# Cross-attention of a two-layer decoder: each head scaled and added to x by one VectorE operation from PSUM, in place of scaled heads in SBUF and a tree of sums on GpSimd

## The chip, the cores and the metric

The kernel runs on one core of one Trainium2 chip. The metric is the device time of one execution in microseconds, lower is better. Before the change the median of three runs is 790.59 us (788.66 to 793.35).

## The reference, cut to what matters

The program is a decoder of two layers on x of 8 batch items x 128 tokens x 128 channels. Each layer has three sublayers, each added to x: a state-space mixer or self-attention, a cross-attention, and a mixture of experts. The change is in the cross-attention, which both layers have. For each item and each of the 16 heads it computes

```python
attn = jax.nn.softmax(scores, axis=-1)
out = jnp.einsum('bhqk,bhkd->bhqd', attn, v)
out = out.transpose(0, 2, 1, 3).reshape(B, NQ, INNER)
return out @ w_out + b_out
```

and the result is added to x. In layer 1 a second, small attention over 4 image tokens is added to `out` ahead of the output product.

## The kernel before, in words

Each sublayer is a block in which all engines start together and which ends when all are done. All data of x (`pg.x`, 8 items of 128x128) stays in SBUF; the next block, the feed-forward, begins with the statistics of all items of x on VectorE.

`cross_attention` folds the value and output weights of each head into one 128-wide matrix, so that a head's output is already 128 channels of x: `vo` holds, for an item, 16 heads x (128 channels and two columns of ones). The product of the unnormalised softmax weights `pt` with `vo[head]` gives in PSUM a head's 128 output channels and, in column 128, its sum of weights. What is left is to divide each head by its sum, add the 16 heads, the bias and x.

A loop over j (items 0 to 7) does item j's second half together with projections and scores of items j + 1, j + 2. The 16 heads are taken in six groups, of 3, 3, 2, 3, 3 and 2 heads (`groups`, `first`), that alternate between the two PSUM banks of `av`: groups 0 to 2, then the transposed scores and exponentials of the second half (`scores_t(j, 2)`), then groups 3 to 5. TensorE's `outputs(j, g)` waits until the group two before it, k - 2, has been read from its bank. All engines work in program order and meet by semaphores, of which the order is written out by hand in the functions of each engine.

VectorE's `normalise` (L1243 to L1258) takes a group's reciprocals (L1248), then multiplies the whole group into the tile `o` (L1254, `o_done`). Behind groups 0 to 2 stands the norm of item j + 3, behind groups 3 to 5 the statistics of item j + 4 and the row maxima of item j + 2 (L1212), which free the banks of the scores. GpSimd adds the 16 heads in a tree (L892 to L906: part, total, total, ...) and the result to x (L911). In layer 1 VectorE adds the image part to x from PSUM behind group 5 (L1257).

Of the kernel before, what the change touches and what calls it, by code (L numbers as in the profile page):

```python
# [10 lines left out]
ALU = mybir.AluOpType  # L11
# [3 lines left out]
P = 128  # L15
NB = 8
D = 128
# [788 lines left out]
def cross_attention(pg, layer):  # L806
# [5 lines left out]
    with ExitStack() as ctx:  # L812
        (split_ready, var_ready, rstd_ready, norm_order, xn_ready, proj_ready, proj_read, wvt_ready, wvt_copied, g_ready,
         g_high_done, g_low_done, c_high_done, c_low_done, ones_done, s_ready, s_read, nm_ready, st_ready, exp_done, av_ready,
         rinv_done, o_done, img_out_added, half_done, sum_order, x_done) = pg.sems(f"ca{layer}", (
            "split_ready var_ready rstd_ready norm_order xn_ready proj_ready proj_read wv_transposed wv_t_copied g_ready "
            "g_high g_low c_high c_low ones_done s_ready s_read max_ready st_ready exp_done av_ready "
            "rinv_done o_done image_added half_summed sum_order x_done"))
# [13 lines left out]
        rinv, o = some(2, "rinv", [P, NH]), some(2, "o", [P, NH, D])  # L832
        part, total = sb("part", [P, 4, D]), sb("total", [P, 4, D])
# [37 lines left out]
        def _(pool):  # L871
# [15 lines left out]
            for j in range(NB):  # L887
                if j + 3 < NB:
                    rstd(j + 3)
                oj = o[j % 2]  # L890
                pool.wait_ge(o_done, NG * j + 3)
                nc.gpsimd.tensor_tensor(part[:, :, :], oj[:, 0:4, :], oj[:, 4:8, :], ALU.add).then_inc(half_done, 1)  # L892
                pool.wait_ge(o_done, NG * j + NG)
                if j:
                    pool.wait_ge(x_done, j)
                s = 5 * j
                nc.gpsimd.tensor_tensor(total[:, :, :], oj[:, 8:12, :], oj[:, 12:16, :], ALU.add).then_inc(sum_order, 1)  # L897
                pool.wait_ge(half_done, j + 1)
                pool.wait_ge(sum_order, s + 1)
                nc.gpsimd.tensor_tensor(total[:, :, :], total[:, :, :], part[:, :, :], ALU.add).then_inc(sum_order, 1)  # L900
                pool.wait_ge(sum_order, s + 2)
                nc.gpsimd.tensor_tensor(total[:, 0:2, :], total[:, 0:2, :], total[:, 2:4, :], ALU.add).then_inc(sum_order, 1)
                pool.wait_ge(sum_order, s + 3)
                nc.gpsimd.tensor_tensor(total[:, 0, :], total[:, 0, :], total[:, 1, :], ALU.add).then_inc(sum_order, 1)
                pool.wait_ge(sum_order, s + 4)
                nc.gpsimd.tensor_tensor(total[:, 0, :], total[:, 0, :], w["bias"][:, :], ALU.add).then_inc(sum_order, 1)  # L906
                pool.wait_ge(sum_order, s + 5)
                pool.wait_ge(xn_ready, j + 1)
                if layer:
                    pool.wait_ge(img_out_added, j + 1)  # L910
                nc.gpsimd.tensor_tensor(pg.x[:, j, :], pg.x[:, j, :], total[:, 0, :], ALU.add).then_inc(x_done, 1)  # L911

        @block.tensor
        def _(pe):
# [91 lines left out]
            def outputs(j, g):  # L1006
                k = NG * j + g
                if k >= 2:
                    pe.wait_ge(o_done, k - 1)
# [180 lines left out]
        def _(dve):  # L1190
# [52 lines left out]
            def normalise(j, g):  # L1243
                dve.wait_ge(av_ready, NG * j + g + 1)
                slots = slice(groups[g][0], groups[g][-1] + 1)
                size = len(groups[g])
                src = av[g % 2][:, 0:size * (D + 2)].rearrange("p (h e) -> p h e", e=D + 2)
                V.reciprocal(rinv[j % 2][:, slots].unsqueeze(2), src[:, :, D:D + 1]).then_inc(rinv_done, 1)  # L1248
                dve.wait_ge(rinv_done, NG * j + g + 1)
                if g == 0 and j >= 2:  # L1250
                    dve.wait_ge(half_done, j - 1)
                if g == 2 and j >= 2:
                    dve.wait_ge(sum_order, 5 * (j - 2) + 1)
                V.tensor_tensor(o[j % 2][:, slots, :], src[:, :, 0:D], bc(rinv[j % 2][:, slots].unsqueeze(2), [P, size, D]),  # L1254
                                ALU.mult).then_inc(o_done, 1)
                if layer and g == NG - 1:
                    V.tensor_tensor(pg.x[:, j, :], av[g % 2][:, 2 * (D + 2):2 * (D + 2) + D], pg.x[:, j, :],  # L1257
                                    ALU.add).then_inc(img_out_added, 1)  # L1258
# [844 lines left out]
```

## Time and profile before

| | |
|---|---|
| median of three runs | 790.59 us (788.66 to 793.35) |
| the profiled execution, its own time | 789.37 us |
| its span, first to last instruction | 787.6 us |
| TensorE busy | 672.5 us (85%) |
| VectorE busy | 391.5 us (50%) |
| ScalarE busy | 289.6 us (37%) |
| GpSimd busy | 194.2 us (25%) |
| mean granted TensorE clock | 0.902 of full |

The busy shares are means over stages with different limits. The cross-attention of layer 0 lies from about 115 to 256 us of the span and that of layer 1 from about 480 to 625 us. What the change is worth is read there: from what TensorE waits for in an item, and from what works last at the end of the block. In the rows DVE is VectorE, PE TensorE's matmuls, PEld its weight loads, ACT ScalarE, POOL GpSimd; a start and a length are in us.

### The profile page before, as it was taken

The numbers are of one execution on the slowest core, as the hardware profiler recorded it, in microseconds if no ns is written. First come the engines' busy times: TensorE is split into PE (matmuls) and PEld (weight loads), VectorE is DVE, ScalarE is ACT, GpSimd is POOL, SyncE is SP. The second block draws the span as 40 slices with busy tenths as digits, with TensorE's granted clock in tenths as the row PEclk, the third lists the DMA queues.
The fourth block names the chain that finished last, engine by engine and source line by source line (L and its number), as shares of the span: only waits on it lengthen the run. The fifth ranks groups of instructions, "written<-read, shape, count | busy, mean of one in ns | idle before, by whom it ended". The sixth has DMA issues, their size and how long they took to land. (4 is left out here: it accounts for less than half of the span.)

```text
span 787.6 us, 13686 instructions
## 1 busy us (share of the span) xinstructions
PE 672.5 (85%) x5200; PEld 554.2 (70%) x5200; DVE 391.5 (50%) x1034; ACT 289.6 (37%) x561; POOL 194.2 (25%) x263
## 2 busy tenths in 40 slices
PE   4395978999995799997899977899998399999997
PEld 2263556888884678886666656788887279999886
DVE  2348754454553655553565524356555354443443
ACT  2443314545442333222444324444543153232331
POOL 8306341243445100002010001034433521111110
PEclk9755978999999699998899958799999879999999
DMA  7800000000000111000000000000000111111110
GB/s 191 198 1 0 0 0 2 1 2 1 2 1 1 41 41 31 30 20 1 2 2 1 2 1 1 1 2 2 2 1 2 44 38 41 40 40 40 43 38 27
DMA packets 23461, 18.33 MB, mean 23 GB/s; under 512 B 5576, under 2 KB 20208, under 8 KB 23408
## 3 DMA queue, kind: packets, MB, share of 16 engines
q1 hardware_dynamic: 23408, 17.60, 8.1%
q8 instruction: 36, 0.59, 0.3%
q14 instruction: 17, 0.14, 0.1%
HBM read 16.68 MB, written 0.52 MB: 22 GB/s over the span
## 5 line engine op out<-in xcount | busy, mean ns | idle before, releaser
L1969 ACT ACTIVATE sb_ff_s<-bank 128x512 f32<-128x512 f32 x96 | 57.4, 598 | 145.4 <-PE bank L1892 144.9
L2038 DVE TENSOR_TENSOR sb_ff_h<-sb_ff_s,bank 128x512 f32<-128x512 f32 x96 | 66.0, 688 | 72.4 <-ACT sb_ff_s L1969 71.1
L1902 PEld LDWEIGHTS bank<-sb_ff_down,sb_ff_h 128*128 128x128 f32 x768 | 88.2, 192 | 1.3
L1902 PE MATMUL bank<-sb_ff_down,sb_ff_h 128*128 128x128 f32 x768 | 88.3, 275 | 0.0
L1892 PE MATMUL bank<-sb_ff_xt_high,sb_ff_low 128*128 128x512 f32 x192 | 79.0, 411 | 1.3 <-DVE sb_ff_h L2038 1.3
L1015 PE MATMUL bank<-sb_ca_vo,sb_ca_pt 128*128 128x130 f32 (+1 forms) x512 | 70.8, 281 | 7.8 <-ACT sb_ca_pt L1133 4.3
L1892 PE MATMUL bank<-sb_ff_xt_low,sb_ff_high 128*128 128x512 f32 x192 | 76.4, 398 | 0.0
L1892 PE MATMUL bank<-sb_ff_xt_high,sb_ff_high 128*128 128x512 f32 x192 | 76.4, 398 | 0.0
L1015 PEld LDWEIGHTS bank<-sb_ca_vo,sb_ca_pt 128*128 128x128 f32 (+1 forms) x512 | 64.2, 190 | 14.4 <-DVE sb_ca_o L1254 7.0
L2031 DVE SCALAR_TENSOR_TENSOR sb_x<-bank,sb_ff_cw,sb_x 128x128 f32<-128x128 f32 x128 | 36.0, 344 | 47.9 <-PE bank L1902 47.9
L1133 ACT ACTIVATE sb_ca_pt<-bank 128x512 f32<-128x512 f32 (+1 forms) x64 | 36.0, 594 | 63.8 <-PE bank L1001 63.8
L1212 DVE TENSOR_REDUCE sb_ca_m<-bank 128x4 f32<-128x512 f32 (+1 forms) x64 | 40.6, 676 | 31.5 <-PE bank L979 31.5
L1117 ACT COPY sb_ca_vo<-bank 128x512 f32<-128x512 f32 (+1 forms) x64 | 37.6, 587 | 50.6 <-PE bank L948 49.0
L1248 DVE RECIPROCAL sb_ca_rinv<-bank 128x3 f32<-128x3 f32 (+1 forms) x96 | 16.7, 174 | 76.9 <-PE bank L1015 68.8
L1254 DVE TENSOR_TENSOR sb_ca_o<-bank,sb_ca_rinv 128x384 f32<-128x384 f32 (+1 forms) x96 | 49.2, 513 | 3.3
L1852 POOL TENSOR_TENSOR sb_ff_low<-sb_ff_gate_up,sb_ff_high 128x1024 fp32r<-128x1024 f32 x8 | 19.2, 2400 | 108.5 <-ACT sb_ff_high L1947 108.5
L1892 PEld LDWEIGHTS bank<-sb_ff_xt_high,sb_ff_low 128*128 128x128 f32 x192 | 37.1, 193 | 9.3 <-DVE sb_ff_h L2038 2.1
L1892 PEld LDWEIGHTS bank<-sb_ff_xt_high,sb_ff_high 128*128 128x128 f32 x192 | 36.8, 192 | 8.4
L1892 PEld LDWEIGHTS bank<-sb_ff_xt_low,sb_ff_high 128*128 128x128 f32 x192 | 37.1, 193 | 7.1
L897 POOL TENSOR_TENSOR sb_ca_total<-sb_ca_o 128x512 f32<-128x512 f32 x16 | 20.3, 1269 | 84.3 <-DVE sb_ca_o L1254 84.3
L936 PE MATMUL bank<-sb_ctx_t,sb_c_k 96*128 96x128 f32 x256 | 35.9, 299 | 5.5 <-PEq L117 3.2
L936 PEld LDWEIGHTS bank<-sb_ctx_t,sb_c_k 96*128 96x128 f32 x256 | 33.1, 209 | 7.0 <-issue 3.7
(339 smaller groups left out, 1231.2 us busy)
## 6 DMA issues: line engine op xcount, KB each, us to landing
sb_ff_w<-in_L_ffn_w_dram SPq DMA_DIRECT2D x8, 256.0 KB, 2.8
sb_ff_gate_up<-in_L_ffn_w_gate_dram SPq DMA_DIRECT2D x8, 256.0 KB, 2.7
sb_ff_gate_up<-in_L_ffn_w_up_dram SPq DMA_DIRECT2D x8, 256.0 KB, 3.0
sb_ff_down<-in_L_ffn_w_down_dram SPq DMA_DIRECT2D x8, 256.0 KB, 3.8
sb_ff_w<-in_L_ffn_w_dram SPq DMA_DIRECT2D x8, 128.0 KB, 2.7
sb_x<-in_x_dram SPq DMA_DIRECT2D x1, 512.0 KB, 5.0
sb_c_q<-in_L_xattn_w_q_dram SPq DMA_DIRECT2D x1, 512.0 KB, 4.7
sb_c_o<-in_L_xattn_w_out_dram SPq DMA_DIRECT2D x1, 512.0 KB, 7.9
```

The lines of the kernel that those rows point to most:

```text
L897: nc.gpsimd.tensor_tensor(total[:, :, :], oj[:, 8:12, :], oj[:, 12:16, :], ALU.add).then_inc(sum_order, 1)
L936: mm = nc.tensor.matmul(proj[h][:, t * P:(t + 1) * P], w["k"][:, (4 * h + t) * P:(4 * h + t + 1) * P], pg.ctx_t[:, n, :], start=True, stop ...
L1015: mm = nc.tensor.matmul(av[g % 2][:, i * (D + 2):(i + 1) * (D + 2)], pt[0:KS, c, r * P:(r + 1) * P], vo[j % 2][0:KS, head(c, r), :], start ...
L1117: nc.scalar.copy(vo[n % 2][0:KS, 4 * q:4 * q + 4, 0:D], proj[q % 2][0:KS, :].rearrange("p (h d) -> p h d", d=D)).then_inc(proj_read, 1)
L1133: nc.scalar.activation(pt[0:KS, c, :], score_t[c % 2][0:KS, :], ACT.Exp).then_inc(exp_done, 1)
L1212: V.tensor_reduce(m[n % 2][:, heads_of(c)], s[:, :, 0:KS], AX, ALU.max, negate=True).then_inc(s_read, 1)
L1254: V.tensor_tensor(o[j % 2][:, slots, :], src[:, :, 0:D], bc(rinv[j % 2][:, slots].unsqueeze(2), [P, size, D]), ALU.mult).then_inc(o_done, 1)
L1892: mm = nc.tensor.matmul(ps[k % BK][:, :], wp[p][:, g, t * P:(t + 1) * P], xs[xp][:, cols], start=(q == 0), stop=(q == 2))
L1902: mm = nc.tensor.matmul(y_ps[n][:, b * D:(b + 1) * D], h[n][:, t, b * P:(b + 1) * P], down[p][:, t, :], start=(t == 0), stop=(t == FT - 1))
L1969: nc.scalar.activation(s[k % BK][:, :], gate_ps[k % BK][:, :], ACT.Silu).then_inc(act_done, 1)
L2031: ins = V.scalar_tensor_tensor(pg.x[:, n * TB + b, :], y_ps[n][:, b * D:(b + 1) * D], cw[:, e, n * TB + b:n * TB + b + 1], pg.x[:, n * TB ...
L2038: V.tensor_tensor(h[k // FT][:, k % FT, :], s[k % BK][:, :], up_ps[k % BK][:, :], ALU.mult).then_inc(h_done, 1)
```

## The change

VectorE's `normalise` becomes `accumulate`: after a group's reciprocals it issues, for each head of the group, one operation that reads the head from PSUM, multiplies it with the head's reciprocal and adds it to x[j], in place. As each reads what the one before wrote, it waits on the semaphore `summed` of the one before. TensorE's `outputs` waits on `summed` up to the last head of group k - 2 (in place of `o_done`). GpSimd's tree goes; it adds the bias to x[j] as soon as the norm of item j has been read (`xn_ready`), and the first group of an item waits for this (`bias_added`). The tiles `o`, `part` and `total` go.

```diff
@@ -885,30 +884,11 @@
             rstd(2)
             pg.wait_loads(pool, f"cross{layer}")
             for j in range(NB):
+
+                pool.wait_ge(xn_ready, j + 1)
+                nc.gpsimd.tensor_tensor(pg.x[:, j, :], pg.x[:, j, :], w["bias"][:, :], ALU.add).then_inc(bias_added, 1)
                 if j + 3 < NB:
                     rstd(j + 3)
-                oj = o[j % 2]
-                pool.wait_ge(o_done, NG * j + 3)
-                nc.gpsimd.tensor_tensor(part[:, :, :], oj[:, 0:4, :], oj[:, 4:8, :], ALU.add).then_inc(half_done, 1)
-                pool.wait_ge(o_done, NG * j + NG)
-                if j:
-                    pool.wait_ge(x_done, j)
-                s = 5 * j
-                nc.gpsimd.tensor_tensor(total[:, :, :], oj[:, 8:12, :], oj[:, 12:16, :], ALU.add).then_inc(sum_order, 1)
-                pool.wait_ge(half_done, j + 1)
-                pool.wait_ge(sum_order, s + 1)
-                nc.gpsimd.tensor_tensor(total[:, :, :], total[:, :, :], part[:, :, :], ALU.add).then_inc(sum_order, 1)
-                pool.wait_ge(sum_order, s + 2)
-                nc.gpsimd.tensor_tensor(total[:, 0:2, :], total[:, 0:2, :], total[:, 2:4, :], ALU.add).then_inc(sum_order, 1)
-                pool.wait_ge(sum_order, s + 3)
-                nc.gpsimd.tensor_tensor(total[:, 0, :], total[:, 0, :], total[:, 1, :], ALU.add).then_inc(sum_order, 1)
-                pool.wait_ge(sum_order, s + 4)
-                nc.gpsimd.tensor_tensor(total[:, 0, :], total[:, 0, :], w["bias"][:, :], ALU.add).then_inc(sum_order, 1)
-                pool.wait_ge(sum_order, s + 5)
-                pool.wait_ge(xn_ready, j + 1)
-                if layer:
-                    pool.wait_ge(img_out_added, j + 1)
-                nc.gpsimd.tensor_tensor(pg.x[:, j, :], pg.x[:, j, :], total[:, 0, :], ALU.add).then_inc(x_done, 1)
 
         @block.tensor
         def _(pe):
@@ -1006,7 +986,7 @@
             def outputs(j, g):
                 k = NG * j + g
                 if k >= 2:
-                    pe.wait_ge(o_done, k - 1)
+                    pe.wait_ge(summed, NH * ((k - 2) // NG) + first[(k - 2) % NG + 1])
                 if layer and g == 1 and j:
                     pe.wait_ge(img_out_added, j)
                 pe.wait_ge(exp_done, NCH * j + groups[g][-1] // HPC + 1)
@@ -1240,20 +1220,22 @@
                 V.tensor_tensor(s2[n % 2][:, :, :], s2[n % 2][:, :, :], bc(sum2[n % 2][:, :].unsqueeze(2), [P, NH, IPA]),
                                 ALU.mult).then_inc(p2_ready, 1)
 
-            def normalise(j, g):
+            def accumulate(j, g):
+
                 dve.wait_ge(av_ready, NG * j + g + 1)
+                if g == 0:
+                    dve.wait_ge(bias_added, j + 1)
                 slots = slice(groups[g][0], groups[g][-1] + 1)
-                size = len(groups[g])
-                src = av[g % 2][:, 0:size * (D + 2)].rearrange("p (h e) -> p h e", e=D + 2)
+                src = av[g % 2][:, 0:len(groups[g]) * (D + 2)].rearrange("p (h e) -> p h e", e=D + 2)
                 V.reciprocal(rinv[j % 2][:, slots].unsqueeze(2), src[:, :, D:D + 1]).then_inc(rinv_done, 1)
                 dve.wait_ge(rinv_done, NG * j + g + 1)
-                if g == 0 and j >= 2:
-                    dve.wait_ge(half_done, j - 1)
-                if g == 2 and j >= 2:
-                    dve.wait_ge(sum_order, 5 * (j - 2) + 1)
-                V.tensor_tensor(o[j % 2][:, slots, :], src[:, :, 0:D], bc(rinv[j % 2][:, slots].unsqueeze(2), [P, size, D]),
-                                ALU.mult).then_inc(o_done, 1)
+                for i, s in enumerate(groups[g]):
+                    if s:
+                        dve.wait_ge(summed, NH * j + s)
+                    V.scalar_tensor_tensor(pg.x[:, j, :], src[:, i, 0:D], rinv[j % 2][:, s:s + 1], pg.x[:, j, :], ALU.mult,
+                                           ALU.add).then_inc(summed, 1)
                 if layer and g == NG - 1:
+                    dve.wait_ge(summed, NH * j + NH)
                     V.tensor_tensor(pg.x[:, j, :], av[g % 2][:, 2 * (D + 2):2 * (D + 2) + D], pg.x[:, j, :],
                                     ALU.add).then_inc(img_out_added, 1)
 
```

In the diff TensorE's hunk is that of `outputs`. The calls of `normalise(j, g)` in VectorE's loop become `accumulate(j, g)` at the same places.

VectorE's instructions of groups 0 to 2 of item 3, layer 0, then the norm of item 6 and the reciprocals of group 3 (the line numbers of the changed kernel are 18 to 20 lower here), before:

```order
L1248 RECIPROCAL sb_ca_rinv<-bank 128x3
L1254 TENSOR_TENSOR sb_ca_o<-bank,sb_ca_rinv 128x384
L1248 RECIPROCAL sb_ca_rinv<-bank 128x3
L1254 TENSOR_TENSOR sb_ca_o<-bank,sb_ca_rinv 128x384
L1248 RECIPROCAL sb_ca_rinv<-bank 128x2
L1254 TENSOR_TENSOR sb_ca_o<-bank,sb_ca_rinv 128x256
L1206 TENSOR_SCALAR sb_ca_xn<-sb_x,sb_ca_mv,sb_ca_rs 128x128
L1248 RECIPROCAL sb_ca_rinv<-bank 128x3
```

and in the changed kernel:

```order
L1230 RECIPROCAL sb_ca_rinv<-bank 128x3
L1235 SCALAR_TENSOR_TENSOR sb_x<-bank,sb_ca_rinv,sb_x 128x128 x3
L1230 RECIPROCAL sb_ca_rinv<-bank 128x3
L1235 SCALAR_TENSOR_TENSOR sb_x<-bank,sb_ca_rinv,sb_x 128x128 x3
L1230 RECIPROCAL sb_ca_rinv<-bank 128x2
L1235 SCALAR_TENSOR_TENSOR sb_x<-bank,sb_ca_rinv,sb_x 128x128 x2
L1186 TENSOR_SCALAR sb_ca_xn<-sb_x,sb_ca_mv,sb_ca_rs 128x128
L1230 RECIPROCAL sb_ca_rinv<-bank 128x3
```

Each 384- or 256-wide multiply into `o` has become three or two 128-wide operations on x; nothing else has changed its place.

GpSimd's instructions in layer 0, the reciprocal root of item 4 (sb_ca_rs) and then the tree of item 1, before:

```order
L874 TENSOR_TENSOR sb_ca_rs<-sb_ca_ve,sb_neg_half 128x1
L892 TENSOR_TENSOR sb_ca_part<-sb_ca_o 128x512
L897 TENSOR_TENSOR sb_ca_total<-sb_ca_o 128x512
L900 TENSOR_TENSOR sb_ca_total<-sb_ca_total,sb_ca_part 128x512
L902 TENSOR_TENSOR sb_ca_total<-sb_ca_total 128x256
L904 TENSOR_TENSOR sb_ca_total<-sb_ca_total 128x128
L906 TENSOR_TENSOR sb_ca_total<-sb_ca_total,sb_c_bias 128x128
L911 TENSOR_TENSOR sb_x<-sb_x,sb_ca_total 128x128
```

and in the changed kernel, from the reciprocal root of item 3 to that of item 5, with the bias of items 1 and 2 between them:

```order
L873 TENSOR_TENSOR sb_ca_rs<-sb_ca_ve,sb_neg_half 128x1
L889 TENSOR_TENSOR sb_x<-sb_x,sb_c_bias 128x128
L873 TENSOR_TENSOR sb_ca_rs<-sb_ca_ve,sb_neg_half 128x1
L889 TENSOR_TENSOR sb_x<-sb_x,sb_c_bias 128x128
L873 TENSOR_TENSOR sb_ca_rs<-sb_ca_ve,sb_neg_half 128x1
```

The seven operations of an item have become one, which waits for no head. Within item j the tree stood behind the reciprocal root of item j + 3; the bias stands ahead of it.

## Rows read from the trace of the kernel before

**Rows 1.** Busy time by stage, steady part of layer 0 (columns in the first row)

```profile
core 0: us, PE busy (x) PEld busy (x) DVE busy (x) ACT busy (x) POOL busy (x), PEclk, DMA share, GB/s
...
160.00:250.00 90.00, 82.94 (x826) 72.17 (x824) 43.89 (x126) 39.40 (x76) 38.44 (x46) 1.00 0.01 2
```

**Rows 2.** TensorE's waits, 140 to 266 us: total, times, longest

```profile
PE bank L1015 <- DVE sb_ca_o L1254: 1.7, 9, 0.2
```

**Rows 3.** Timeline, layer 0, item 3, first half: start, length, engine, line [idle before]

```profile
189.81 0.18 DVE L1248 RECIPROCAL sb_ca_rinv<-bank 128x3 f32<-128x3 f32 x1 [0.53 <-PE bank L1015]
190.03 0.56 DVE L1254 TENSOR_TENSOR sb_ca_o<-bank,sb_ca_rinv 128x384 f32<-128x384 f32 x1
190.50 0.17 DVE L1248 RECIPROCAL sb_ca_rinv<-bank 128x3 f32<-128x3 f32 x1
...
190.64 0.71 PE L1015 MATMUL bank<-sb_ca_vo,sb_ca_pt 128*128 128x130 f32 x4 [0.20 <-DVE sb_ca_o L1254]
...
191.28 1.16 PE L996 MATMUL bank<-sb_ca_qt,sb_ca_kt 64*128 64x128 f32 x16
...
192.70 1.08 ACT L1133 ACTIVATE sb_ca_pt<-bank 128x512 f32<-128x512 f32 x2 [2.97 <-PE bank L1001]
```

**Rows 4.** Timeline, the same item, second half, and the row maxima behind it

```profile
196.37 0.18 DVE L1248 RECIPROCAL sb_ca_rinv<-bank 128x3 f32<-128x3 f32 x1 [4.10 <-PE bank L1015]
...
197.31 0.65 PEld L1015 LDWEIGHTS bank<-sb_ca_vo,sb_ca_pt 128*128 128x128 f32 x4
197.54 0.61 PE L1015 MATMUL bank<-sb_ca_vo,sb_ca_pt 128*128 128x130 f32 x4
...
197.90 0.48 PE L948 MATMUL bank<-sb_ca_g_high,sb_ca_c_low 96*128 96x512 f32 x1
...
199.34 1.28 DVE L1212 TENSOR_REDUCE sb_ca_m<-bank 128x4 f32<-128x512 f32 x2
...
202.27 0.40 PE L979 MATMUL bank<-sb_ca_kt,sb_ca_qt 64*128 64x128 bf16 x8
```

**Rows 5.** Timeline, end of layer 0's cross-attention (item 7)

```profile
248.21 0.18 DVE L1248 RECIPROCAL sb_ca_rinv<-bank 128x3 f32<-128x3 f32 x1 [2.37 <-PE bank L1015]
...
249.03 0.71 PE L1015 MATMUL bank<-sb_ca_vo,sb_ca_pt 128*128 128x130 f32 x4 [0.19 <-DVE sb_ca_o L1254]
...
255.11 0.45 POOL L911 TENSOR_TENSOR sb_x<-sb_x,sb_ca_total 128x128 f32<-128x128 f32 x1
...
255.94 1.64 DVE L221 BATCH_NORM_STATS2 sb_ff_st<-sb_x 128x6 f32<-128x128 f32 x8
```

**Rows 6.** Timeline, end of layer 1's cross-attention (item 7)

```profile
617.11 0.18 DVE L1248 RECIPROCAL sb_ca_rinv<-bank 128x3 f32<-128x3 f32 x1 [2.35 <-PE bank L1015]
...
619.65 0.28 DVE L1257 TENSOR_TENSOR sb_x<-bank,sb_x 128x128 f32<-128x128 f32 x1
...
624.43 0.45 POOL L911 TENSOR_TENSOR sb_x<-sb_x,sb_ca_total 128x128 f32<-128x128 f32 x1
```

**Rows 7.** Scale and add in the feed-forward: durations ns min/median/max; one run of four

```profile
L2031 DVE SCALAR_TENSOR_TENSOR sb_x<-bank,sb_ff_cw,sb_x x128: 340/343/352, 278.5 to 783.4; 128x128 f32<-128x128 f32 x128
...
278.52 1.13 DVE L2031 SCALAR_TENSOR_TENSOR sb_x<-bank,sb_ff_cw,sb_x 128x128 f32<-128x128 f32 x4 [0.59 <-PE bank L1902]
```

**Rows 8.** Timeline of VectorE in the routing of the first feed-forward

```profile
268.52 0.69 DVE L2016 TENSOR_TENSOR sb_ff_gt<-sb_ff_pr 128x512 f32<-128x512 f32 x1
269.13 0.68 DVE L2017 TENSOR_TENSOR sb_ff_eq<-sb_ff_pr 128x512 f32<-128x512 f32 x1
269.85 0.69 DVE L2018 TENSOR_TENSOR sb_ff_eq<-sb_ff_eq,sb_ff_lower 128x512 f32<-128x512 f32 x1
```

**Rows 9.** Granted clock in the pause (columns as in Rows 1), and TensorE after it

```profile
253.50:254.50 1.00, 0.00 (x0) 0.00 (x0) 0.00 (x0) 0.00 (x0) 0.92 (x2) 0.70 0.00 0
...
259.51 1.11 PE L1880 MATMUL bank<-sb_ident,sb_ff_w 128*128 128x128 f32 x4 [1.78 <-DMA sb_ff_w<-in_L_ffn_w_dram]
...
263.12 3.55 PE L1919 MATMUL bank<-sb_ff_w_router,sb_ff_xt 128*128 128x8 f32 x16 [0.34 <-ACT sb_ff_xt_high L1962]
```

More of the change, by code:

```diff
@@ L814, in cross_attention @@
          g_high_done, g_low_done, c_high_done, c_low_done, ones_done, s_ready, s_read, nm_ready, st_ready, exp_done, av_ready,
-         rinv_done, o_done, img_out_added, half_done, sum_order, x_done) = pg.sems(f"ca{layer}", (
+         rinv_done, bias_added, img_out_added, summed) = pg.sems(f"ca{layer}", (
             "split_ready var_ready rstd_ready norm_order xn_ready proj_ready proj_read wv_transposed wv_t_copied g_ready "
             "g_high g_low c_high c_low ones_done s_ready s_read max_ready st_ready exp_done av_ready "
-            "rinv_done o_done image_added half_summed sum_order x_done"))
+            "rinv_done bias_added image_added summed"))
         if layer:
@@ L831, in cross_attention @@
         pt = sb("pt", [P, NCH, HPC * P])
-        rinv, o = some(2, "rinv", [P, NH]), some(2, "o", [P, NH, D])
-        part, total = sb("part", [P, 4, D]), sb("total", [P, 4, D])
+        rinv = some(2, "rinv", [P, NH])
         if layer:
@@ L1293, in _ @@
                 for g in range(3):
-                    normalise(j, g)
+                    accumulate(j, g)
                 if j + 3 < NB:
@@ L1299, in _ @@
                 for g in range(3, 6):
-                    normalise(j, g)
+                    accumulate(j, g)
                 if layer and ahead < NB:
```

## The prediction

> **What bounds the kernel now.** I read the busy table by stage first. In the steady part of the first cross-attention TensorE is busy 82.94 of 90 us while VectorE is busy 43.89 and GpSimd 38.44 [rows 1], so TensorE's own order of work is the clock of the stage, and the other engines matter only where TensorE waits for them. Next I read the list of TensorE's waits: for VectorE's normalised heads it waits nine times, 1.7 us in all [rows 2]. That is small, but the change makes just this wait longer, so I looked at where it sits.
>
> The timeline of one batch item (item 3 of layer 0) shows it. The `av` groups alternate between two banks, so group 2 can't be multiplied before group 0 has been read. VectorE takes the reciprocals of group 0 at 189.81, multiplies from 190.03 for 0.56 us, and TensorE starts group 2 at 190.64, that is 0.83 us after the reciprocal's start and 0.05 after the multiply's end [rows 3]. Right behind those four products stand the transposed scores of the second half (191.28), and the exponentials of ScalarE wait for these (192.70, idle 2.97 before) [rows 3]. TensorE needs the exponentials, then, for group 3. So a delay at group 2 is passed on by the whole item, and nothing in it takes it up.
>
> In the second half group 5 waits in the same way for group 3. There the bank was free in time: reciprocal of group 3 at 196.37, weights of group 5 loaded ahead from 197.31, products at 197.54, 1.17 us after the reciprocal, and the next product at 197.90 [rows 4].
>
> At the stage's end only GpSimd works: its tree of sums ends at 255.11 + 0.45 = 255.56, and the next stage's statistics start at 255.94 [rows 5]. From the reciprocal of group 3 (248.21) that is 7.35 us. In layer 1 it is 624.43 + 0.45 - 617.11 = 7.77 us [rows 6].
>
> **What the change adds in the middle of the stage.** A group's one multiply becomes three (or two) operations that scale a head from PSUM and add it to x, each of which reads the x that the one before wrote and waits for it. The trace has this very operation and shape in the feed-forward: 343 ns [rows 7]. There four of them without waits take 1.13 us, a pace of (1.13 - 0.343) / 3 = 0.26 us [rows 7]. What a wait between them costs is seen on two neighbours in the routing: L2016 and L2017 don't depend on each other and start 0.61 us apart at 0.69 us each, L2018 needs L2017 (0.68 us) and starts 0.72 after it [rows 8]. So a dependent step costs its duration and about 0.04, here 0.38 us, and loses the 0.08 of overlap. I take 0.38; the ends for the range are 0.26 (the pace without waits) and 0.45 (0.38 and a delay of two more such hand-overs, for reading back a row of x that was only just written, which no row shows).
>
> Group 0: reciprocal 0.22 (189.81 to 190.03), two steps of 0.38, the last 0.343, hand-over 0.05, together 1.37 us against 0.83. TensorE loses 0.54 us in each item, 16 items in two layers: **+8.7 us**.
>
> Group 3: the bank is free 1.37 us after the reciprocal, 0.20 later than TensorE comes for it now (1.17). Besides, TensorE then waits with its weights not loaded. From a release to the next product four such matmuls take 0.64 (190.64 to 191.28) [rows 3], with weights loaded ahead 0.36 (197.54 to 197.90) [rows 4]. So the loss is between 0.20 and 0.48; I take 0.35. It counts in items 0 to 6 of both layers (in item 7 the chain on VectorE is the end itself): 14 x 0.35 = **+4.9 us**.
>
> VectorE needs 1.24 us for a group of three (0.22 + 0.76 + 0.343 less 0.08 of overlap) and 0.93 for the last, of two: 3.41 us from the reciprocal of group 3. The row maxima, which stand behind, began 2.97 us after it (199.34) and ended at 200.62; they now begin about 1 us later, TensorE about 0.35 later. TensorE needs their banks at 202.27 [rows 4], so some 1 us of the 1.65 us of cover is left: cost nothing. If the cover is gone, each microsecond that VectorE is late beyond it costs one per item. The norm of item j + 3 and, in layer 1, the image softmax stand in the same queue and have longer cover, as their readers on TensorE come after the scores or in the next item.
>
> **What it takes away.** The tree (part, total and their sums) leaves GpSimd. In the steady part nobody waits for it. At the ends it is the path: VectorE's chain ends 3.41 us after the reciprocal of group 3 instead of 7.35, **-3.9 us** in layer 0; in layer 1 the image part is added to x behind it (0.28 [rows 6] and 0.04), 3.73 against 7.77, **-4.0 us**. The bias is added by GpSimd ahead of its use; x has been read by the norm by then, and the first group comes long after: nothing.
>
> **The sum.** 8.7 + 4.9 - 7.9 = +5.7 us. The profiled execution took 789.37 us (span 787.6), so 795.1; it lies 1.2 below the median of the three runs, from which it would be 796.3. I say **795.5 us**, 0.6% slower. One hundredth of a microsecond in the step moves the total by 0.7 us (32 + 28 + 10 steps in series), so the step's price is the thing to get right.
>
> The Trainium skill speaks against the price I give the wait. "VectorE: DVE Perf Modes", section "The DRAIN you can't avoid", says that a semaphore after each operation costs nothing extra, since the next one doesn't start before the pipe is empty anyway. By that rule a wait changes nothing, and the sum is that of the first rival below. The trace disagrees, with 0.61 against 0.72 us from start to start [rows 8].
>
> The same page, section on the TRN2 errata, gives 120 cycles and one per element for an operation from PSUM. An estimate from it would be 0.26 us for 128 elements, a step of 0.30 and a sum near zero; the trace has 343 ns for the operation itself [rows 7], and that is used.
>
> **Rivals.**
> (a) *The chain runs at the pace without waits, 0.26 us a step* (ends on the other side). Group 0: 0.22 + 0.52 + 0.343 + 0.05 = 1.13, so +0.30 x 16 = 4.8; group 3 is then in time (1.13 < 1.17), 0; the end of the stage takes 1.00 + 1.00 + 0.81 = 2.81, so -4.5 and -4.6. Sum -4.3: 785 to 786.5 us. The turning point, where the sum is zero, is a step of about 0.30 to 0.31. For it: each operation waits in VectorE's own queue, in order. Against: dependent pairs cost their duration and about 0.04 more, the long one of [rows 8] as well as the reciprocal and the multiply of [rows 3]. Chance 0.08.
> (b) *The clock stays up over the end of the stage.* The last matmul of layer 0 ends at 249.03 + 0.71 = 249.74 [rows 5]; between 253.5 and 254.5 the granted clock averages 0.70, so it fell near 253.9, 4.2 us into the pause, from 2.4 to 1.2 GHz [rows 9]. The transposes come at 259.51, a pause of 9.8 us [rows 9], which shrinks to about 5.3. By the row it still falls, but with 1 us to spare. If it does not, the 3.55 us of router matmuls [rows 9] take about half, -1.8 us in layer 0, and as much again in layer 1. Then 792 to 793.5 us. Chance 0.2, with steps a little cheaper than mine counted in.
> (c) *The steps cost more*, 0.45 us, or VectorE gets so late that the row maxima hold TensorE. 0.07 x 70 = +4.9: about 800 us. For it: nothing in the trace reads and writes the same row in a chain from PSUM. Against: the pairs seen behave alike. Chance 0.1.
> (d) *The end of the stage was hidden anyway*, so that nothing is given back: 803 us. Against it: VectorE and TensorE stand idle there until the tree is done [rows 5]. Chance 0.02.
> The forecast, with sums from +2.5 to +8.5 us, has 0.6.
>
> **Numbers.** The forecast alone spans 793 to 799. The bounds of the step and rival (b) widen it to 790 to 800 for 8 in 10. What a measurement of this kernel tells from no change is about 0.5%, here 786.6 and 794.5. Faster: rival (a), 0.08. Same: rival (b) and the lower quarter of the forecast, 0.34. Slower: the rest, 0.58.
>
> **What would show it.** In the new profile: operations of 343 ns on sb_x, 0.38 us apart in a group; TensorE's wait for group 2 near 0.75 us instead of 0.20 in every item, and a new wait before group 5 of 0.2 us or more; an item of layer 0 about 0.9 us longer; no GpSimd at the stage's end, and the feed-forward's statistics some 3.8 us after the reciprocal of group 3 of the last item. The prediction is wrong if the steps start 0.26 or over 0.42 apart, if the row maxima make the scores wait, or if the clock doesn't fall before the feed-forward.

## The result, and the profile after

The changed kernel takes 795.47 us (median of 13 executions) against 789.45 us before (13 executions on the same chips): ratio 1.006, 95% interval 1.0036 to 1.0084. One execution of the changed kernel, of 1574.77 us, and one of the two sums below, of 3424.86 us, are left out of the ratios but not of the medians (without the first, the changed kernel's median is 794.87 us). The change makes the kernel 0.6% slower, as forecast (795.5 us).

The page of the profiled execution (its own time 793.11 us) gives the span and the busy time of each engine:

```profile
span 791.3 us, 13776 instructions
...
PE 673.2 (85%) x5200; PEld 550.5 (70%) x5200; DVE 426.4 (54%) x1194; ACT 289.8 (37%) x561; POOL 106.4 (13%) x167
```

The same page among the costliest groups (busy time, mean ns of one, idle time before them and what ended it):

```profile
L1235 DVE SCALAR_TENSOR_TENSOR sb_x<-bank,sb_ca_rinv,sb_x 128x128 f32<-128x128 f32 x256 | 89.8, 351 | 9.4 <-DVE sb_ca_rinv L1230 0.4
...
L995 PE MATMUL bank<-sb_ca_vo,sb_ca_pt 128*128 128x130 f32 (+1 forms) x512 | 72.3, 284 | 18.9 <-DVE sb_x L1235 13.7
```

GpSimd lost 88 us of work and VectorE gained 35. Neither says much. What counts is the last number: TensorE's output products now stood idle 13.7 us, over both layers, for VectorE's operations on x. The busy time of the steady part of layer 0, and TensorE's waits from 140 to 266 us:

```profile
160.00:250.00 90.00, 80.51 (x783) 68.29 (x781) 55.41 (x178) 39.03 (x76) 3.78 (x8) 1.00 0.01 2
```

```profile
PE bank L995 <- DVE sb_x L1235: 6.8, 9, 0.8
...
PE bank L959 <- DVE sb_ca_m L1192: 0.3, 1, 0.3
```

Against [rows 1] TensorE does 2.4 us less in the same 90 us, at the full clock (1.00). Against [rows 2] the nine waits have grown from 1.7 to 6.8 us in all. The scores (L959) waited for the row maxima once, for 0.3 us, where they waited once for 0.2 before. The place is item 5:

```profile
237.33 0.40 PE L959 MATMUL bank<-sb_ca_kt,sb_ca_qt 64*128 64x128 bf16 x7 [0.32 <-DVE sb_ca_m L1192]
```

In the other items of this layer the cover held.

Item 3 of layer 0 in the timeline, first half, which answers to [rows 3]:

```profile
193.43 0.18 DVE L1230 RECIPROCAL sb_ca_rinv<-bank 128x3 f32<-128x3 f32 x1 [0.53 <-PE bank L995]
193.64 1.12 DVE L1235 SCALAR_TENSOR_TENSOR sb_x<-bank,sb_ca_rinv,sb_x 128x128 f32<-128x128 f32 x3
...
194.82 0.71 PE L995 MATMUL bank<-sb_ca_vo,sb_ca_pt 128*128 128x130 f32 x4 [0.76 <-DVE sb_x L1235]
...
195.46 1.16 PE L976 MATMUL bank<-sb_ca_qt,sb_ca_kt 64*128 64x128 f32 x16
...
196.88 1.08 ACT L1113 ACTIVATE sb_ca_pt<-bank 128x512 f32<-128x512 f32 x2 [3.53 <-PE bank L981]
```

Three operations take 1.12 us, so they start (1.12 - 0.351) / 2 = 0.385 us apart. Group 2 starts 1.39 us after the reciprocal of group 0 (before: 0.83), and the 0.56 us come back in full where ScalarE waits for the scores of the second half: its idle time before the exponentials grew from 2.97 to 3.53 us. The second half of the item, which answers to [rows 4]:

```profile
200.55 0.18 DVE L1230 RECIPROCAL sb_ca_rinv<-bank 128x3 f32<-128x3 f32 x1 [3.44 <-PE bank L995]
...
201.94 0.52 PEld L995 LDWEIGHTS bank<-sb_ca_vo,sb_ca_pt 128*128 128x128 f32 x4 [0.50 <-DVE sb_x L1235]
201.95 0.71 PE L995 MATMUL bank<-sb_ca_vo,sb_ca_pt 128*128 128x130 f32 x4
...
202.41 0.48 PE L928 MATMUL bank<-sb_ca_g_high,sb_ca_c_low 96*128 96x512 f32 x1
...
204.51 1.28 DVE L1192 TENSOR_REDUCE sb_ca_m<-bank 128x4 f32<-128x512 f32 x2
```

Here too TensorE now comes before the bank is free. Its matmuls show no wait, but its weight loads (PEld) do, 0.50 us: weights that were loaded ahead at 197.31 in [rows 4] are now loaded when the bank is free. Who reads only the matmuls' waits misses this one.

The end of layer 0's cross-attention, which answers to [rows 5], with the start of the feed-forward:

```profile
257.42 0.17 DVE L1230 RECIPROCAL sb_ca_rinv<-bank 128x3 f32<-128x3 f32 x1
...
258.86 0.74 DVE L1235 SCALAR_TENSOR_TENSOR sb_x<-bank,sb_ca_rinv,sb_x 128x128 f32<-128x128 f32 x2
...
259.94 1.64 DVE L221 BATCH_NORM_STATS2 sb_ff_st<-sb_x 128x6 f32<-128x128 f32 x8
...
267.06 3.55 PE L1901 MATMUL bank<-sb_ff_w_router,sb_ff_xt 128*128 128x8 f32 x16 [0.28 <-ACT sb_ff_xt_high L1944]
```

No GpSimd stands between the last head and the statistics, which start at 259.94. The reciprocal of group 3 of item 7 stood at 256.16, so that is 3.78 us, where [rows 5] have 255.94 - 248.21 = 7.73.

### The stages, from marks in the timeline

Executions of one kernel scatter by several microseconds (before: 783.1 to 793.8 us), so each kernel below is also read by marks in its timeline: from the reciprocal of group 0 of item 0 to that of item 7 (seven items), and from there to the statistics of the feed-forward (item 7), in each layer. The last column is the sum of the four, less that of the kernel before. It is worked out from start times in the timeline. Where two kernels have the same form in a column, the marks agree to 0.07 us (99.29 and 99.28, 105.75 and 105.74, 12.31 and 12.30), so they repeat far better than whole times. The lead-in of each cross-attention, before the first mark, is not in the sum: from its first statistics to the first reciprocal it takes 28.5 to 29.1 us in layer 0 in eight of the ten kernels (31.9 and 33.1 in "two sums" and "last only, short"), and 36.3 to 37.2 us in layer 1, in no order by form.

| kernel | 7 items, layer 0 | item 7 | 7 items, layer 1 | item 7 | against before |
|---|---|---|---|---|---|
| before | 99.29 | 12.31 | 105.87 | 12.71 | |
| changed | 105.75 | 8.92 | 112.04 | 9.30 | +5.83 |
| last item only | 99.28 | 8.93 | 105.80 | 9.31 | -6.86 |
| all but the last | 105.74 | 12.30 | 112.07 | 12.70 | +12.63 |
| two sums | 102.11 | 8.35 | 108.65 | 8.99 | -2.08 |
| short first group | 102.98 | 8.75 | 109.20 | 9.12 | -0.13 |
| last only, short | 98.29 | 8.76 | 104.83 | 9.13 | -9.17 |
| before, short | 98.29 | 12.38 | 104.88 | 12.78 | -1.85 |
| two sums, short | 100.22 | 8.31 | 106.76 | 8.94 | -5.95 |
| last group behind | 103.66 | 8.92 | 110.53 | 9.30 | +2.23 |

In the four kernels with a short first group the first mark itself comes 0.22 us earlier, as group 0 has two heads to multiply and not three (from its first product to its reciprocal 0.65 us in place of 0.87). That cancels between items and lengthens both item 7 columns, so their sums are some 0.4 us too high.

The changed kernel takes 6.46 and 6.17 us more in the items and 3.39 and 3.41 less at the ends: +5.83 us. The two profiled executions differ by 793.11 - 789.37 = +3.74 us, so 2.1 us came back outside the stages, where but for the bias both run the same code. One stretch there, from the first expert matmul of the first feed-forward to the start of the second cross-attention, is 4.8 us shorter (199.06 in place of 203.87), and three others are longer by 0.9 each: the part ahead of the first mark, the second lead-in, and the part behind the last mark. The windows table shows what goes with the shorter stretch (columns as in [rows 1]; before, then changed):

```profile
430.00:480.00 50.00, 42.77 (x409) 30.85 (x409) 20.02 (x46) 16.86 (x37) 5.26 (x9) 0.73 0.01 1
```

```profile
430.00:480.00 50.00, 42.10 (x470) 30.48 (x471) 22.29 (x53) 19.09 (x43) 6.16 (x11) 0.86 0.01 1
```

The granted clock is 0.73 in one and 0.86 in the other. That is not the change's doing: of the experiments, whichever form their cross-attention has, six take 203.4 to 203.8 us here, at 0.73 in this window, and two 199.0 to 199.1, at 0.88 and 0.86 (all but the last, and two sums with a short group).

### The profile page after: what moved, and what is told of

The parts are those of the page before. It is cut to its first block and busy times, and to the rows that moved or that the text cites. A ratio compares the mean times of both kernels' runs of the same rounds, so it can differ in the third digit from the quotient of the medians.

```text
span 791.3 us, 13776 instructions
## 1 busy us (share of the span) xinstructions
PE 673.2 (85%) x5200; PEld 550.5 (70%) x5200; DVE 426.4 (54%) x1194; ACT 289.8 (37%) x561; POOL 106.4 (13%) x167
## 5 line engine op out<-in xcount | busy, mean ns | idle before, releaser
L1235 DVE SCALAR_TENSOR_TENSOR sb_x<-bank,sb_ca_rinv,sb_x 128x128 f32<-128x128 f32 x256 | 89.8, 351 | 9.4 <-DVE sb_ca_rinv L1230 0.4
L995 PE MATMUL bank<-sb_ca_vo,sb_ca_pt 128*128 128x130 f32 (+1 forms) x512 | 72.3, 284 | 18.9 <-DVE sb_x L1235 13.7
L1874 PEld LDWEIGHTS bank<-sb_ff_xt_high,sb_ff_low 128*128 128x128 f32 x192 | 37.2, 194 | 9.3 <-DVE sb_ff_h L2020 2.1
L916 PEld LDWEIGHTS bank<-sb_ctx_t,sb_c_k 96*128 96x128 f32 x256 | 33.1, 209 | 7.0 <-issue 3.7
L909 PE MATMUL bank<-sb_ca_xt,sb_c_q 128*128 128x128 f32 x256 | 35.9, 298 | 1.3 <-ACT sb_ca_xt L1093 1.3
L976 PE MATMUL bank<-sb_ca_qt,sb_ca_kt 64*128 64x128 f32 (+1 forms) x512 | 37.0, 285 | 0.0
```

The lines of the kernel that those rows point to most:

```text
L916: mm = nc.tensor.matmul(proj[h][:, t * P:(t + 1) * P], w["k"][:, (4 * h + t) * P:(4 * h + t + 1) * P], pg.ctx_t[:, n, :], start=True, stop ...
L976: nc.tensor.matmul(score_t[g][0:KS, r * P:(r + 1) * P], half(kt[j % 3], 2 * c0 + r, g)[:, 0:KS], half(qt[j % 3], 2 * c0 + r, g), start=(r ...
L995: mm = nc.tensor.matmul(av[g % 2][:, i * (D + 2):(i + 1) * (D + 2)], pt[0:KS, c, r * P:(r + 1) * P], vo[j % 2][0:KS, head(c, r), :], start ...
L1235: V.scalar_tensor_tensor(pg.x[:, j, :], src[:, i, 0:D], rinv[j % 2][:, s:s + 1], pg.x[:, j, :], ALU.mult, ALU.add).then_inc(summed, 1)
L1874: mm = nc.tensor.matmul(ps[k % BK][:, :], wp[p][:, g, t * P:(t + 1) * P], xs[xp][:, cols], start=(q == 0), stop=(q == 2))
```

## The experiments

My theory: TensorE loses 0.54 us an item at group 2 and 0.35 at group 5, because each head's operation waits for the result of the one before, 0.38 us a step; the end of the stage gives back 3.9 and 4.0 us. The rivals that the result leaves standing: the same sum could come of other parts (steps at the pace of 0.26 us and a cost elsewhere, for instance in VectorE's longer queue), or of a smaller gain at the ends. Every kernel here computes the whole reference. Ratios are against the kernel before, with their intervals.

### The gain alone: direct sums in item 7 only

```diff
-            for j in range(NB):
+            for j in range(NB - 1):
...
-                    pe.wait_ge(o_done, k - 1)
+                    if k - 2 < NG * (NB - 1):
+                        pe.wait_ge(o_done, k - 1)
+                    else:
+                        pe.wait_ge(summed, first[g - 1])
...
+                if j == NB - 1:
+                    if g == 0:
+                        dve.wait_ge(bias_added, 1)
+                    for i, s in enumerate(groups[g]):
+                        if s:
+                            dve.wait_ge(summed, s)
+                        V.scalar_tensor_tensor(pg.x[:, j, :], src[:, i, 0:D], rinv[j % 2][:, s:s + 1], pg.x[:, j, :],
+                                               ALU.mult, ALU.add).then_inc(summed, 1)
```

> The kernel before, with the direct sum into x in item 7 of both layers alone (items 0 to 6 keep the multiply into o and GpSimd's tree). If the change's two parts are what I take them for, this keeps the whole gain at the stage's end (3.9 + 4.0 us) and pays the longer wait for group 0 only twice (2 x 0.54): -6.8 us against the kernel before, a ratio near 0.991. Rival: the end of the stage was covered by something else (the next stage's loads, the clock), so that no more than a part of the 7.9 us comes back: ratio 0.996 to 1.000. In the profile: in item 7 TensorE's wait for group 2 is 0.76 us, in the others 0.20; the feed-forward's statistics start 3.8 us (layer 0) and 4.2 us (layer 1) after the reciprocal of group 3 of item 7.

Measured: 783.88 us, 0.9951 (0.9925 to 0.9976). In the stages -3.38 and -3.40 us in item 7, -0.01 and -0.07 in the others. The end of layer 0 on VectorE:

```profile
248.68 0.18 DVE L1254 RECIPROCAL sb_ca_rinv<-bank 128x3 f32<-128x3 f32 x1 [1.70 <-PE bank L1021]
248.90 1.12 DVE L1262 SCALAR_TENSOR_TENSOR sb_x<-bank,sb_ca_rinv,sb_x 128x128 f32<-128x128 f32 x3
...
251.38 0.74 DVE L1262 SCALAR_TENSOR_TENSOR sb_x<-bank,sb_ca_rinv,sb_x 128x128 f32<-128x128 f32 x2
...
252.48 0.87 DVE L221 BATCH_NORM_STATS2 sb_ff_st<-sb_x 128x6 f32<-128x128 f32 x4
```

From the reciprocal to the statistics it takes 3.80 us, and 3.78 in the changed kernel. So in the stages the gain at the ends is there, is worth 6.8 us with item 7's own wait for group 2 paid, and needs nothing from the other items. The whole times show less: the interval leaves out the 0.991 that I forecast and holds the lower end of the rival's 0.996 to 1.000. What decides for the gain is the timeline, and where the missing 3 us of the whole time went is taken up below and stays open.

### The cost alone: direct sums in items 0 to 6, the tree in item 7

```diff
+                if j < NB - 1:
+                    pool.wait_ge(xn_ready, j + 1)
+                    nc.gpsimd.tensor_tensor(pg.x[:, j, :], pg.x[:, j, :], w["bias"][:, :], ALU.add).then_inc(bias_added, 1)
+                    if j + 3 < NB:
+                        rstd(j + 3)
+                    continue
+                pool.wait_ge(o_done, 3)
+                nc.gpsimd.tensor_tensor(part[:, :, :], o[:, 0:4, :], o[:, 4:8, :], ALU.add).then_inc(half_done, 1)
...
+                if j == NB - 1:
+                    V.tensor_tensor(o[:, slots, :], src[:, :, 0:D], bc(rinv[j % 2][:, slots].unsqueeze(2), [P, len(groups[g]), D]),
+                                    ALU.mult).then_inc(o_done, 1)
```

> The changed kernel, with item 7 of both layers as before (multiply into o, GpSimd's tree). It keeps the cost in the body of the stage and drops the gain at its end: 14 x (0.54 + 0.35) = +12.5 us against the kernel before, ratio near 1.016. An item of layer 0 takes 16.06 us from group 0 to group 0 in place of 15.16. Rival: the body costs less than that and the end gives less, so that the two only seem to add up: ratio 1.006 to 1.010.

Measured: 802.74 us, 1.0204 (1.016 to 1.0247; four executions). In the stages +6.45 and +6.20 us in the seven items, nothing in item 7. The two halves of the change add up: -6.86 and +12.63 are +5.77, against +5.83 for the whole. So within the stages no hidden third cost is left, and the rival "a smaller gain at the ends" falls.

### The dependence taken out: two running sums

Even heads are added to x, odd heads to a second tile, so that an operation needs the result of the one before the last. Each head still signals, each from the third on waits, and there is one addition more.

```diff
                 for i, s in enumerate(groups[g]):
-                    if s:
-                        dve.wait_ge(summed, NH * j + s)
+                    if s >= 2:
+                        dve.wait_ge(summed, NH * j + s - 1)
+                    part = odd[j % 2][:, :] if s % 2 else pg.x[:, j, :]
...
+                if g == NG - 1:
+                    dve.wait_ge(summed, NH * j + NH)
+                    V.tensor_tensor(pg.x[:, j, :], pg.x[:, j, :], odd[j % 2][:, :], ALU.add).then_inc(merged, 1)
```

> The changed kernel, with two running sums: heads with an even number add into x, those with an odd number into a tile of its own (the first of them only scales), and one more operation per item adds that tile to x. Each operation then waits for the one two before it, so the number of operations on VectorE is 17 per item but neighbours don't depend on each other. If the dependent step (0.385 us measured) is what costs, the steps go at about 0.27 us: group 0 is free 1.15 us after its reciprocal in place of 1.37, group 3 is in time (1.15 against 1.17), and the end of the stage takes about 3.2 us in place of 3.4: 16 x 0.22 + 14 x 0.35 + 0.4 = 8.8 us less than the changed kernel, -2.8 us against the kernel before, ratio near 0.9965. Rival: what costs is the number of operations and their fixed length, not the dependence; the steps stay at 0.35 us or more and the ratio stays at 1.004 to 1.008.

Measured: 788.93 us, 1.0008 (0.9981 to 1.0035). VectorE in the second half of item 3, and TensorE's waits:

```profile
201.36 0.18 DVE L1231 RECIPROCAL sb_ca_rinv<-bank 128x3 f32<-128x3 f32 x1 [3.82 <-PE bank L996]
201.57 0.35 DVE L1240 SCALAR_TENSOR_TENSOR sb_x<-bank,sb_ca_rinv,sb_x 128x128 f32<-128x128 f32 x1
...
201.84 0.34 DVE L1240 SCALAR_TENSOR_TENSOR sb_ca_odd<-bank,sb_ca_rinv,sb_ca_odd 128x128 f32<-128x128 f32 x1
...
202.10 0.34 DVE L1240 SCALAR_TENSOR_TENSOR sb_x<-bank,sb_ca_rinv,sb_x 128x128 f32<-128x128 f32 x1
...
202.53 0.68 PE L996 MATMUL bank<-sb_ca_vo,sb_ca_pt 128*128 128x130 f32 x4
```

```profile
PE bank L996 <- DVE sb_x L1240: 4.5, 9, 0.5
```

The same operation in the same place, with a wait and a signal each time, now starts every 0.265 us ((202.10 - 201.57) / 2), in place of 0.385. So it is not a wait and a signal as such that cost, but having to wait for the operation directly ahead: 0.12 us a step. But every operation here that needs the result of the one directly ahead also waits for that one's semaphore. Which of the two makes the price, the result or the wait on the operation directly ahead, no run separates. Group 5 stands 1.17 us behind the reciprocal again (202.53 - 201.36), as in [rows 4], and the wait for group 2 has shrunk from 0.76 to 0.50 us. The items get back 3.64 and 3.39 us, the ends 0.57 and 0.31. The rival "the steps run at 0.26 and the cost is elsewhere" falls: at that pace an item costs 0.40 us more than before (2.82 / 7), not 0.90. The stages give back 7.9 us where I forecast 8.8, and the ratio of 0.9965 that I forecast lies outside the interval.

### The first group made short

The first bank is free sooner if group 0 has two heads (groups of 2, 3, 3 in the first half in place of 3, 3, 2). In the changed kernel, in the kernel before, with the direct form in item 7 only, and with two sums:

```diff
-        first = (0, 3, 6, 8, 11, 14, 16)
+        first = (0, 2, 5, 8, 11, 14, 16)
```

> The changed kernel with the heads of the first half split 2, 3, 3 in place of 3, 3, 2. Group 0 then has one step less, and its bank is free 0.38 us earlier relative to its last product, while TensorE comes for it at the same distance: its wait before group 2 falls from 0.76 to about 0.37 us in each of 16 items, -6.1 us against the changed kernel, about 0 against the kernel before, ratio 0.997 to 1.001. Rival: the wait is only moved (to the transposed scores, or to group 4, which waits for group 2 with its three heads): the ratio stays near 1.006.

> The kernel before with nothing but the split 2, 3, 3 in the first half. 16 x 0.14 = 2.2 us less: ratio near 0.997. Rival: no effect, because GpSimd's sum of heads 0 to 7 or ScalarE's exponentials hold the item, not the bank: body as before, 99.3 and 105.9 us.

> Item 7 alone in the direct form (as in the first experiment), and in all items the first half's heads split 2, 3, 3. The multiply of a first group of two heads takes 0.42 in place of 0.56 us, so TensorE's wait before group 2 falls from 0.20 to 0.06 in items 0 to 6: 14 x 0.14 = 2.0 us less than the first experiment, and 0.35 more in the two items 7. Stages: each body about 1.0 us shorter than before (98.3 and 104.9), item 7 to the feed-forward 8.8 and 9.1 us. In all 9.1 us less than the kernel before, if nothing outside the stages changes: ratio near 0.9885; by what the first experiment gave in whole executions (0.995 where its stages said 0.991) rather 0.992. Rival: the split only moves the wait to another group and the ratio is that of the first experiment.

> The changed kernel with two running sums and the split 2, 3, 3. Group 0 is free 0.22 + 0.265 + 0.34 + 0.05 = 0.88 us after its reciprocal, TensorE comes 0.63 after it, so the wait is 0.25 us, against 0.50 measured with two sums and 3, 3, 2: 16 x 0.25 = 4.0 us less than that. Stages against the kernel before: bodies +1.1 us each, item 7 about -4 us each: -6 us, ratio near 0.992. Rival: a lower bound from VectorE's load (17 operations an item) shows as a wait for the row maxima.

Measured, changed kernel: 788.13 us, 1.0011 (0.9986 to 1.0036), in the stages 5.96 us less than the changed kernel. Its row of TensorE's waits:

```profile
PE bank L995 <- DVE sb_x L1235: 3.6, 9, 0.8
```

One step fewer ahead of the release takes 0.40 and 0.41 us from each of the seven items (2.77 and 2.84 us), which is close to the step's price of 0.385, read where it bounds TensorE. Item 7 shows 0.17 and 0.18, which is 0.39 and 0.40 with the 0.22 us by which its mark comes earlier.

Measured, kernel before: 789.05 us, 1.0004 (0.9979 to 1.003). In the stages -1.85 us: 0.14 less in each of the seven items, and 0.07 more in item 7, which is 0.15 less when the earlier mark is counted. The small wait of [rows 2] is gone but once:

```profile
PE bank L1015 <- DVE sb_ca_o L1254: 0.2, 1, 0.2
```

The whole time does not show it: I expected a ratio of 0.997, and the interval holds both that and 1. That comparison is too coarse for 2 us.

Measured, direct in item 7 only: 781.24 us, 0.9906 (0.9872 to 0.994), -9.17 us in the stages. This is faster than the kernel before in both readings, and has the lowest stages and the lowest ratio of all; its interval overlaps with those of "last item only" and "two sums, short", so by whole times alone it is not shown to be better than these. Measured, two sums with a short first group: 781.89 us, 0.9942 (0.9913 to 0.997), -5.95 us in the stages; an item is 0.13 us longer than before. Its waits of group 2 are down to 0.24 us, close to the 0.20 of the kernel before:

```profile
PE bank L996 <- DVE sb_ca_odd L1238: 1.9, 8, 0.2
```

### The second term alone: group 5 behind the last projection

TensorE does the last value projection ahead of group 5 in place of behind it, so that group 3 has 0.67 us more to be read.

```diff
                 if n < NB:
                     project_vo(n, 2)
+                    project_vo(n, 3)
                 outputs(j, 5)
                 if n < NB:
-                    project_vo(n, 3)
                     if layer:
```

> The changed kernel with TensorE's order in the second half changed: the last quarter of the next item's values (0.9 us of products, for which it comes anyway) ahead of group 5, not behind it. If the second part of the body's cost is the wait of group 5 for group 3, with its weights not loaded ahead (0.34 us an item measured), it goes: 14 x 0.35 = 4.9 us less than the changed kernel, bodies 103.3 and 109.7 us in place of 105.75 and 112.04, ratio near 1.000. Rival: the 0.34 us an item is something else (ScalarE's copies, the row maxima coming later): the bodies stay within 0.5 us of the changed kernel's. It may cost a little, as ScalarE's copy of those values has to free their bank one step earlier.

Measured: 793.24 us, 1.0056 (1.0028 to 1.0084). The wait is gone; item 2 of layer 0 in the timeline:

```profile
184.41 0.18 DVE L1230 RECIPROCAL sb_ca_rinv<-bank 128x3 f32<-128x3 f32 x1 [3.44 <-PE bank L995]
...
186.02 0.65 PEld L995 LDWEIGHTS bank<-sb_ca_vo,sb_ca_pt 128*128 128x128 f32 x4
186.25 0.61 PE L995 MATMUL bank<-sb_ca_vo,sb_ca_pt 128*128 128x130 f32 x4
...
188.40 0.60 ACT L1113 ACTIVATE sb_ca_pt<-bank 128x512 f32<-128x512 f32 x1 [1.36 <-PE bank L981]
```

The weights are loaded ahead again. The exponentials of the changed kernel, in item 3, whose reciprocal of group 3 stood at 200.55:

```profile
204.89 0.60 ACT L1113 ACTIVATE sb_ca_pt<-bank 128x512 f32<-128x512 f32 x1 [0.92 <-PE bank L981]
```

They start 204.89 - 200.55 = 4.34 us after the reciprocal there and 188.40 - 184.41 = 3.99 us after it here, 0.35 us earlier. The idle time before them grew, from 0.92 to 1.36 us, only because ScalarE's copies of the values, which stand ahead, end earlier still.

In the stages the order gives back 2.09 and 1.51 us, where I forecast 4.9 in all. Measured item by item, from the reciprocal of group 3 to the next item's reciprocal of group 0, layer 0 gets back 0.33 to 0.37 us in six of the seven items (8.93 to 8.58 in the steady ones) and nothing in item 5 (7.38 to 7.39). In layer 1 five items get back 0.24 to 0.38 and item 6 0.43, while item 5 loses 0.36 (8.39 to 8.75). Item 5 is where the scores wait for VectorE's row maxima: the seven products that wait start 4.69 us after the reciprocal of group 3 as they do in the changed kernel (4.68) in layer 0, and 6.08 in place of 5.72 us in layer 1. So the second term is shown, in layer 0 at the size that I took, 0.35 us an item, in layer 1 at 0.26 in the steady items; in item 5 another wait takes the gain up. The whole time does not resolve the 3.6 us: its ratio is that of the changed kernel.

### Stages and whole times

| kernel | stages, us | from the ratio, us |
|---|---|---|
| changed | +5.8 | +4.7 (±1.9) |
| last item only | -6.9 | -3.9 (±2.0) |
| all but the last | +12.6 | +16.1 (±3.4) |
| two sums | -2.1 | +0.6 (±2.1) |
| short first group | -0.1 | +0.9 (±2.0) |
| last only, short | -9.2 | -7.4 (±2.7) |
| before, short | -1.9 | +0.3 (±2.0) |
| two sums, short | -6.0 | -4.6 (±2.2) |
| last group behind | +2.2 | +4.4 (±2.2) |

The right column is (ratio - 1) x 788 us. Each of the eight experiments lies 1.0 to 3.5 us above its stages, the changed kernel 1.1 below. Their order is nearly the same, the level is not. The eight are not eight independent signs. They share one profile of the kernel before and two sets of its executions, with medians of 788.33 and 788.16 us, 1.1 to 1.3 below the 789.45 of the set beside which the changed kernel ran. Besides, a whole time goes with the mean granted clock of its execution: in the first of the two sets the kernel before takes 783.1 to 784.7 us at 0.910 to 0.912 and 789.2 to 790.9 at 0.900 to 0.902, so executions of one kernel lie 5 to 8 us apart, and the clock with them. That leaves up to 2.3 us of the shift unexplained, most of all in "last item only" and "all but the last", and this stays open.

## Why the prediction was right, step by step

**The step.** Taken at 0.38 us from two neighbours in another stage [rows 8]; measured 0.385. The bound of 0.26 is what the operation takes without a direct dependence (0.265 in the two sums), so rival (a) named the right price for the wrong case. The Trainium skill, "VectorE: DVE Perf Modes", section "The DRAIN you can't avoid", says that a semaphore after each operation costs nothing extra, and that the next operation does not start before the pipe is empty. For the semaphore this case's traces agree: two sums have one after each operation and keep 0.265 us. For the start they disagree: an operation of 0.34 to 0.35 us is followed 0.265 later by one that doesn't need it, and 0.385 later by one that does. The same section adds that a next operation that is not held starts earlier, which fits the 0.265.

**Group 0, +8.7 us.** Assumed 1.37 us from reciprocal to products, a loss of 0.54 and a wait near 0.75; measured 1.39, 0.56 and 0.76. Over 16 items +9.0 (the forecast's 16 x 0.54 is 8.6, not 8.7, which changes nothing). The reading that nothing in the item takes the delay up held: ScalarE's idle time grew by the same 0.56 us.

**Group 5, +4.9 us.** From the reciprocal of group 3 to the next item's reciprocal of group 0, a steady item grew from 8.60 to 8.93 us in layer 0 and from 9.27 to 9.61 in layer 1, so by 0.33 and 0.34, where I took 0.35 between 0.20 and 0.48. (From group 0 to group 3 it grew by 0.56 and 0.57, the first term.) Its two parts stand in the timeline of item 3: the products come 201.95 - 200.55 = 1.40 us after the reciprocal in place of 1.17 (0.23), and the next matmul 0.46 behind them in place of 0.36 (0.10). Item 5, where the scores wait for the row maxima, grew by 0.50 in layer 0 and by 0.17 in layer 1. Over 14 items +4.7.

**The end, -7.9 us.** From the reciprocal of group 3 to the statistics 3.78 in place of 7.73 us (-3.95) and in layer 1 4.18 in place of 8.15 (-3.97). Sum of the three: 9.0 + 4.7 - 7.9 = +5.8 us, forecast +5.7, measured in the stages +5.83.

**Costs put at nothing.** The row maxima began 204.51 - 200.55 = 3.96 us after the reciprocal in place of 2.97, the 1 us later that was forecast. In item 5 they do make the scores wait, which the forecast had named as a sign of being wrong; but they did so before the change too, and what item 5 costs beyond the 0.33 us of the others, +0.17 us in layer 0 and -0.17 in layer 1, cancels. The bias on GpSimd held nobody: the profile has no wait of VectorE for it.

**The rivals.** (a) would have given 785 to 786.5 us, 4.3 less than before. The two sums do run at that pace; with their 17th operation their stages are 2.1 us less. (b) The pause of layer 0 shrank (last matmul until 257.56 + 0.71 = 258.27, transposes at 263.46: 5.2 us), and the clock still fell from 2.4 to 1.2 GHz within it. The granted clock of two stretches:

```profile
259.00:261.00 2.00, 0.00 (x0) 0.00 (x0) 1.61 (x9) 0.00 (x0) 0.15 (x1) 1.00 0.01 2
262.00:274.00 12.00, 10.26 (x38) 8.92 (x39) 7.24 (x23) 5.04 (x9) 1.93 (x2) 0.50 0.19 56
```

It is full until 261 and half from 262 on, and the router matmuls take 3.55 us as in [rows 9]. The mean of 0.67 between 261 and 262 puts the fall 3.1 us behind the last matmul, where the rival had taken 4.2 from [rows 9], so its 1 us to spare was no fixed margin. In layer 1 the pause shrank from 10.9 to 6.3 us, and the clock fell 3.5 us into it in both kernels, so nothing was given back there either. (c) fell with the step, (d) with item 7.

**What was lucky.** The median came out 0.03 us from the forecast, but the executions that the ratio counts have a median of 794.87 us, medians of the kernel before lie between 788.2 and 789.5 in three sets of executions, and the ratio's interval is 4 us wide. What the study confirms is the +5.8 us in the stages. There the group 2 term was some 0.4 us too small and the group 5 term 0.2 too large, and that the row maxima of item 5 cost something in one layer and the reverse in the other was not foreseen.

## What to carry to other kernels

A chain of operations on one accumulator paid a price for each link (here 0.12 us on 0.265) that operations with another between them didn't. Before such a chain takes the place of a wide operation, ask who waits for its last link: at the end of a stage, where it replaced a tree on a slower engine, it saved 3.9 us, and in the middle, where it holds the bank that TensorE wants next, it cost 0.9 us an item. Use it where it pays, in the last item only, and make the first group short: 0.9906 of the time before, against 1.006 for the form used everywhere. And when a wait of the matmuls looks small, look at the weight loads too.

## What was unexpected of the hardware

The operation took 351 ns here (349 to 352 over 256), 8 ns more than the median of the same shape in the feed-forward [rows 7]. The difference does not come of the operands. Here and in the feed-forward an operation that starts while another scale-and-add still runs takes 339 to 345 ns, and in the two sums the first of a group, behind the reciprocal that it needs, takes 349 to 353 (0.34 and 0.35 in the rows above). In the changed kernel every one starts behind the end of another.

The same code outside the changed stages took 199.06 or 203.87 us according to where the granted clock fell in it (0.86 or 0.73 over 50 us). That is as large as the effect under study: two profiled executions of kernels that differ by 5.8 us in their stages differed by 3.7. An effect of 2 to 4 us on this kernel can be read from stage marks, and hardly from medians of a dozen executions.
